# A tile's transpose turn in two halves, router turns of two tiles, and a new order at the end of a scan kernel

## The chip, the cores and the metric

The kernel runs on one core of one Trainium2 chip. The metric is the device time of one execution in microseconds (us). Before the change three timed runs gave 1213.72, 1214.86 and 1219.25 us, median 1214.86 us.

## The reference, cut to what matters

The input `x` is 2 sequences of 1024 tokens, 256 wide (2048 tokens). Two layers follow one another; each has a sequence part and a feed-forward part, both on a layer-normed input and with a residual:

```
# layer 0, attention part: a selective scan with state 64
xn    = norm(x) * norm_w + norm_b
proj  = xn @ x_proj_w.T                       # 128 + 64 + 64 columns
delta = softplus(proj[:, :128] @ dt_proj_w.T + dt_proj_b)
for each token:                               # per sequence
    h = exp(delta * A) * h + delta * B * xn   # h: 256 channels x 64 states
    y = sum over states of h * C
x = x + (y + x * D_param) @ out_proj_w.T
# layer 0, feed-forward part: mixture of experts
probs = softmax(norm(x) @ Wg)                 # 8 experts, the best 2 of each token
# place of a token in its expert = rank over all tokens; beyond CAP = 640 it is dropped
x = x + sum over 2 experts of gate * (relu(x_e @ w1[e]) @ w2[e])
# layer 1: linear attention with 16 heads, then a gated feed-forward part (silu)
```

A token's place in an expert depends on all tokens before it, so tokens are routed in order. The first expert can't start before every row that it takes has been written to its slot.

## The kernel before, in words

**Stages.** In the profiled execution the scan runs from about 32 to 626 us, the end of the scan stage with the last routing to about 658 us, the eight experts to about 960 us, and layer 1 to the end. The change is in the first two and in the loads of the first two experts.

**The scan stage.** The 2048 tokens are 32 chunks of 64 (`c`), and each chunk has 8 groups of 16 channels (`j`): 256 groups `gi = 8 c + j`. A tile is 128 tokens, two chunks. For each group TensorE makes the decay exponents (`decays`, L909, for group `gi + 2`) and the scan's inputs (L928); ScalarE takes the exponentials (L1089) and writes the carry of the chunk before into the inputs' first column (`hand_on`, L1097); GpSimd multiplies the carry (L1412 to L1421); VectorE runs one scan instruction of 1024 elements (L1266). TensorE's `stream(gi)` waits until the scan of group `gi - 2` is done, multiplies `unread[gi - 1]` products that nobody reads (`stay_awake`, L895), and then makes the inputs of `gi` and the decays of `gi + 2`.

**The order.** `scan_schedule()` (L619 to L733) writes one list of steps; each engine walks through this list and does its own part of every step, in order. Beside the groups there are: `y` (L944, the state times C, four steps per chunk, in groups 2, 3, 5 and 7), the finish of a tile (`TILE_END`, L566), the projections of later tokens (`unit_steps`, names that begin with `u_`) and the routing of finished tiles (`router_steps`, L576). `unread_after` (L736) counts the TensorE work of a group by `PE_WORK` and gives the group after it 3 unread products less that count, not below 0.

**The turns of bank z.** The eighth PSUM bank serves all side work in turns. A step of `Z_WRITE` opens it (TensorE writes) and its partner closes it (ScalarE or VectorE reads and counts up `z_free`). Router and unit turns open only in groups 4 and 6 of an even chunk and 1 and 3 of an odd one, and not between a tile's `yT` and its `resid`.

**A tile's finish.** `yT` turns the skipped input `xs` and the scan's output `y_sb` of both chunks (L979, L984) in one group, group 5 of an odd chunk; `yt` copies it (L1207, L1208), `proj` and `proj2` multiply by the output weights (L956), `resid` copies to `x1o` (L1215). `skip_in` makes `xs` on GpSimd.

**Routing.** Tiles go in blocks `ROUTED` of 4, 4, 4, 3 and 1 tiles. In a block each tile is transposed in one turn (`tr`, L1032, and `xt`, L1233) and multiplied by the router's weights in the next (`mm`, L1052), and ScalarE copies its logits away. Then come top 2 (`CHOOSE`), the gates (`WEIGH`), the ranks, the slots (`SETTLE`) and two indirect DMAs per tile from GpSimd (`scatter`, L1483). Block 2 (tiles 8 to 11) has its eight scatters from group 255 on. Blocks 3 (tiles 12 to 14) and 4 (tile 15) are routed after the last group in an order written out by hand (L707 to L733), in other banks.

**Behind the scan.** SP loads the weights of experts 0 and 1 (`load_experts`, 4 MB) behind the last group, waits for all scatters, and then loads the rows of expert 0 (L1673). TensorE runs `IDLE_ROUTED` = 14 unread products of 512 columns in the meantime (L553), so that the experts' first transposes (L1556) come next in its queue.

Of the kernel before, what the change touches and what calls it, by code (L numbers as in the profile page):

```python
# [7 lines left out]
P = 128  # L8
# [3 lines left out]
ALU = mybir.AluOpType  # L12
ACT = mybir.ActivationFunctionType
# [533 lines left out]
IDLE_ROUTED = 14  # L547
# [28 lines left out]
def router_steps(blk):  # L576
# [36 lines left out]
Z_WRITE = {"tr": "xt", "mm_last": "logit", "rank": "pick", "yT": "yt", "proj": "resid", "first": "first_out",  # L613
# [5 lines left out]
def scan_schedule():  # L619
# [7 lines left out]
    def stamp(name, *args):  # L627
# [8 lines left out]
        if name in ("mm", "proj2"):  # L636
            return (name, *args, z)
        return (name, *args)

    def advance(work, c=CHUNKS, j=4):  # L640
        if work:
# [3 lines left out]
            if steps[0] and steps[0][0][0] == "u_dt" and j > GROUPS - 3:  # L645
                return
# [19 lines left out]
    for gi in range(TOTAL + LAG):  # L666
# [8 lines left out]
        yield from advance(units, c, j)  # L675
        yield from advance(routing, c, j)
        if c >= CHUNKS - 4 and routing and not any(name in AT_PACE for name, *args in routing[0][1][0]):
            yield from advance(routing, c, j)
# [30 lines left out]
    yield ("skip_in", TILES - 1)  # L709
# [7 lines left out]
    yield stamp("yT", TILES - 1)  # L717
    yield stamp("yt", TILES - 1)
# [30 lines left out]
def selective_scan(k, a, s):  # L749
    pe, act, dve, pool, sp, sem = k.pe, k.act, k.dve, k.pool, k.sp, k.sem  # L750
    ident, eps, slots = s["ident"], s["eps"], s["slots"]
    with ExitStack() as ctx:
# [3 lines left out]
        logit_, top_, less_, prob_ = (sb("r_" + n, [P, NR, EXPERTS]) for n in ("logit", "top", "less", "prob"))  # L756
        hot_, own_ = sb("r_hot", [P, NR, 2, EXPERTS]), sb("r_own", [P, NR, 2, EXPERTS])
        xt = sb("r_xt", [P, 2, DH, P])
# [57 lines left out]
        xt_of = lambda blk, i: (last_xt[:, NR - 1 if blk == len(ROUTED) - 1 else i] if blk in ends else xt[:, i % 2])  # L816

        def on_sp():
# [8 lines left out]
            for kind, *x in schedule:  # L827
# [1485 lines left out]
```

## Time and profile before

| what | us |
|---|---|
| median of three timed runs | 1214.86 |
| profiled execution, device time | 1209.28 |
| its span, first to last instruction | 1207.7 |
| TensorE busy in the span | 1087.6 (90%) |
| VectorE busy | 761.2 (63%) |
| ScalarE busy | 519.3 (43%) |
| GpSimd busy | 323.7 (27%) |
| VectorE busy from 60 to 660 us | 561.02 of 600 |
| mean granted TensorE clock | 0.979 |

Busy time is the time in which an engine had an instruction under way. A mean over the span mixes stages: up to about 626 us VectorE is busy nearly all the time, behind 660 us TensorE is. Rows of the timeline give start, length, engine, line, operation and shape, and in square brackets how long the engine was idle before it and what ended that. Ends of matmuls are modelled.

### The profile page before, as it was taken

How to read it: one execution, taken by the hardware profiler on the slowest of the kernel's cores; microseconds unless marked ns; L12 is line 12 of the kernel's file. 1: busy time of each engine (PE TensorE's matmuls, PEld its weight loads, DVE VectorE, ACT ScalarE, POOL GpSimd, SP SyncE). 2: the span in 40 equal slices, each digit the busy share in tenths (PEclk: the TensorE clock that was granted, in tenths of full speed). 3: DMA queues.
4: the chain of work that ended last, by engine and by line, in shares of the span. 5: the costliest groups of instructions: out<-in, count | busy, mean ns of one | idle time of the engine just before them, and what ended most of it. 6: DMA issues, size and time to landing. Idle time of an engine off the chain costs nothing. (4 is left out here: it accounts for less than half of the span.)

```text
span 1207.7 us, 30229 instructions
## 1 busy us (share of the span) xinstructions
PE 1087.6 (90%) x12351; PEld 735.4 (61%) x12351; DVE 761.2 (63%) x874; ACT 519.3 (43%) x1344; POOL 323.7 (27%) x949
## 2 busy tenths in 40 slices
PE   3889888889888899888878999999999899999998
PEld 2655555556555565555544877788867666576465
DVE  5999999999999999999972112111111667242111
ACT  3777776776766767666541111111112212112110
POOL 5344444343345424443242110111111210000000
PEclk7899999999998999998998999999999999999999
DMA  6767747342353533523217622232110400000000
GB/s 159 165 161 175 176 107 197 64 109 74 77 123 86 119 66 70 126 62 71 37 56 273 258 107 102 74 110 109 56 47 20 140 1 1 1 18 9 9 18 18
DMA packets 183899, 110.11 MB, mean 91 GB/s; under 512 B 95517, under 2 KB 178336, under 8 KB 181408
## 3 DMA queue, kind: packets, MB, share of 16 engines
q1 hardware_dynamic: 178816, 98.65, 31.6%
q0 software_dynamic: 3456, 8.48, 2.0%
q8 instruction: 97, 1.59, 0.6%
q10 hardware_dynamic: 1488, 1.05, 0.4%
q14 instruction: 42, 0.34, 0.1%
HBM read 63.25 MB, written 43.90 MB: 89 GB/s over the span
## 5 line engine op out<-in xcount | busy, mean ns | idle before, releaser
L1266 DVE TENSOR_TENSOR_SCAN h<-decay,psum 128x1024 f32<-128x1024 f32 x256 | 564.8, 2266 | 18.1 <-ACT psum L1097 10.5
L1089 ACT ACTIVATE decay<-psum 128x512 f32<-128x512 f32 x512 | 278.6, 598 | 45.9 <-PE psum L909 43.0
L928 PEld LDWEIGHTS psum<-xdiag,bstat 128*128 128x128 bf16 x4096 | 148.4, 99 | 112.4 <-DVE h L1266 76.5
L928 PE MATMUL psum<-xdiag,bstat 128*128 128x64 bf16 x4096 | 166.5, 195 | 13.1 <-DVE h L1266 12.0
L1581 PE MATMUL psum<-shared,hid 128*128 128x256 f32 x640 | 139.7, 379 | 0.9 <-DVE hid L1660 0.9
L944 PE MATMUL psum<-h,cstat 128*32 128x512 f32 x1024 | 138.2, 614 | 2.3 <-DVE h L1266 1.7
L1569 PE MATMUL psum<-xdt,shared 128*128 128x320 f32 (+2 forms) x512 | 139.5, 433 | 0.8 <-ACT xdt L1632 0.8
L1581 PEld LDWEIGHTS psum<-shared,hid 128*128 128x128 f32 x640 | 120.9, 190 | 17.7 <-issue 1.7
L895 PE MATMUL psum<-shared 128*128 128x512 bf16 x262 | 74.3, 390 | 60.0 <-DVE h L1266 59.9
L1569 PEld LDWEIGHTS psum<-xdt,shared 128*128 128x128 f32 x512 | 92.3, 190 | 45.2 <-issue 15.3
L909 PE MATMUL psum<-rows,shared 32*128 32x64 bf16 x4096 | 106.0, 191 | 12.3 <-DMA rows<-parts_d 9.0
L1412 POOL TENSOR_TENSOR carry<-decay,h 128x16 f32<-128x16 f32 x240 | 58.1, 242 | 203.8 <-ACT decay L1089 201.6
L2190 PE MATMUL psum<-xt,wgu 128*128 128x512 f32 x256 | 110.6, 592 | 0.0
L1693 POOL DMA_INDIRECT picked_d<-eo,to x40 | 38.9, 972 | 255.2 <-ACT eo L1629 152.9
L1660 DVE TENSOR_SCALAR hid<-psum 128x320 f32<-128x320 f32 (+1 forms) x56 | 29.1, 520 | 103.9 <-PE psum L1569 103.9
L909 PEld LDWEIGHTS psum<-rows,shared 32*128 32x128 bf16 x4096 | 75.4, 94 | 27.1 <-issue 10.8
L1097 ACT COPY psum<-carry 128x16 f32<-128x16 f32 x240 | 43.4, 181 | 109.9 <-PE psum L928 90.6
L2190 PEld LDWEIGHTS psum<-xt,wgu 128*128 128x128 f32 x256 | 48.6, 190 | 59.7 <-issue 59.5
L1626 ACT ACTIVATE hid<-psum 128x320 f32<-128x320 f32 (+2 forms) x72 | 30.2, 419 | 117.7 <-PE psum L1569 117.7
L1663 DVE TENSOR_SCALAR eo<-psum,gate 128x256 f32<-128x256 f32 x19 | 9.2, 484 | 112.9 <-PE psum L1581 107.2
L1963 DVE TENSOR_TENSOR shared<-psum,sil 128x512 f32<-128x512 f32 x32 | 22.1, 690 | 86.0 <-PE psum L2190 86.0
L1418 POOL TENSOR_TENSOR carry<-carry,u 128x16 f32<-128x16 f32 x240 | 52.9, 220 | 84.2 <-ACT u L1126 67.7
(245 smaller groups left out, 1086.9 us busy)
## 6 DMA issues: line engine op xcount, KB each, us to landing
shared<-in_w SPq DMA_DIRECT2D x16, 1024.0 KB, 4.8
xdiag<-x_parts_d SPq DMA_DIRECT2D x124, 96.0 KB
rows<-parts_d SPq DMA_DIRECT2D x128, 48.0 KB
x_parts_d<-x_parts SPq DMA_DIRECT2D x14, 384.0 KB, 3.4
x_parts_d<-x_parts SPq DMA_DIRECT2D x21, 256.0 KB, 3.3
disp_d<-r_xl SPq DMA_DIRECT2D x4, 1305.0 KB, 8.5
xd<-disp_d SPq DMA_DIRECT2D x8, 652.5 KB, 6.1
picked_d<-r_xl SPq DMA_DIRECT2D x4, 1024.0 KB, 5.5
```

The costliest lines, as they stand in the source:

```text
L895: pe.q.matmul(bank, s["astat"][:, 0, :], s["astat"][:, 0:4, :].rearrange("p c m -> p (c m)"), start=True, stop=True)
L909: ins = pe.q.matmul(bank_a[half][:, i * T:(i + 1) * T], s["astat"][strip, RCH * g + q, :], rows[strip, c % 2, q, :], start=True, stop=True)
L928: ins = pe.q.matmul(to.rearrange("p d (s e) -> p s d e", e=2), bstat[:, c % 2, b, :], xdiag[:, c % 2, b, :, d, :], start=True, stop=True)
L944: ins = pe.q.matmul(bank_y[32 * q:32 * q + 32, :].rearrange("p (s d e) -> p s d e", s=2, e=4), s["cstat"][:, tok // 4, :], h[:, first:last ...
L1089: act.q.activation(decay[:, gi % NB, 8 * half:8 * half + 8, :], per_d(bank_a[half]), ACT.Exp).then_inc(sem("exp"), 1)
L1097: act.q.copy(per_d(bank_in[gi % 2])[:, :, 0], carry[:, gi % NB, :]).then_inc(sem("handed_on"), 1)
L1266: dve.q.tensor_tensor_scan(out=h[:, half_slot(c, half), ch:ch + G, :].rearrange("p d t -> p (d t)"), data0=decay[:, gi % NB, :, :].rearran ...
L1412: pool.q.tensor_tensor(whole, first, h[:, half_slot(c - 1, half), ch:ch + G, T - 1], ALU.mult).then_inc(sem("carry_made"), 1)
L1418: pool.q.tensor_tensor(whole.rearrange("p (h i) -> p h i", h=2), whole.rearrange("p (h i) -> p h i", h=2), own, ALU.add).then_inc(sem("car ...
L1569: ins = pe.q.matmul(table.bank(key)[:, 0:cols.stop - cols.start], w1[:, e % 2, dh, f * P:(f + 1) * P], xdt[:, e % 2, dh, cols], start=dh = ...
L1581: ins = pe.q.matmul(table.bank(key)[:, 0:D], hid[:, e % 2, f, st * P:(st + 1) * P], w2[:, e % 2, f, :], start=f == 0, stop=f == FT - 1)
L2190: ins = pe.q.matmul(table.bank(key)[:, :], wgu[:, j, dh, f * P:(f + 1) * P], xt[:, u, dh, :], start=dh == 0, stop=dh == 1)
```

## The change

It has five parts.

- `yT` does the first chunk of a tile in group 4 of the odd chunk, and a new step `yT2` the second in group 5. `PE_WORK` counts each as 2, so the unread products ahead of group 5 go from 3 to 1. A unit's `u_dt` no longer opens in group 3 of an odd chunk.
- Router turns take two tiles: `tr` makes four transposes and `xt` one copy of 512 columns; one `mm` step multiplies all tiles of the block (8 matmuls for 4 tiles), an empty step follows, and VectorE copies all logits at once. `PE_WORK` counts `tr` as 4; `mm` is not in it.
- Behind the last group: `skip_in` of tile 15 comes right after group 256's step instead of behind the eight scatters of block 2; blocks 3's `exp`, gates, slots and scatters come ahead of `resid` of tile 15 and of block 4.
- SP loads only `w1` of expert 0 behind the last group; the other three loads stand behind the experts' row loads.
- `IDLE_ROUTED` goes from 14 to 10. Some small tiles are shared (`r_less` with `r_prob`, `r_own` with `r_hot`), and `r_xt` has room for four tiles.

```diff
-IDLE_ROUTED = 14
+IDLE_ROUTED = 10
-PE_WORK = {"y": 4, "u_turn": 4, "u_proj": 6, "u_dt": 4, "u_tx": 4, "tr": 2, "yT": 4, "proj": 4}
+PE_WORK = {"y": 4, "u_turn": 4, "u_proj": 6, "u_dt": 4, "u_tx": 4, "tr": 4, "yT": 2, "yT2": 2, "proj": 4}
-TILE_END = ((4, 4, "yT"), (5, 5, "yt"), (8, 6, "proj"), (8, 6, "proj2"), (10, 8, "resid"))
+TILE_END = ((3, 3, "yT"), (4, 4, "yT2"), (5, 5, "yt"), (8, 6, "proj"), (8, 6, "proj2"), (10, 8, "resid"))
@@ router_steps
-    for i in range(n):
-        yield ([("mm", i - 1)] if i else []) + [("tr", i)]
+    for i in range(0, n, 2):
+        yield [("tr", i)]
         yield [("xt", i)]
-    yield [("mm_last", n - 1)]
+    yield [("mm",)]
+    yield []
@@ scan_schedule
-            if steps[0] and steps[0][0][0] == "u_dt" and j > GROUPS - 3:
+            if steps[0] and steps[0][0][0] == "u_dt" and (j > GROUPS - 3 or (c % CT and j == 3)):
...
+        if gi == TOTAL:
+            yield ("skip_in", TILES - 1)
...
-    yield from ((name, b3) for name in CHOOSE if name != "exp")
+    yield from ((name, b3) for name in CHOOSE)
     yield ("rank", b3)
+    yield from ((name, b3) for name in (*WEIGH, *SETTLE))
+    yield from (("scatter", b3, i, j) for i in range(ROUTED[b3][1]) for j in range(2))
     yield stamp("resid", TILES - 1)
     yield from ((name, b4) for name in NORM)
-    yield ("exp", b3)
+    yield ("count", b3)
     yield from (("turn", b4), ("turned", b4), ("score", b4, 0))
-    yield from ((name, b3) for name in (*WEIGH, *SETTLE, "count"))
-    yield from (("scatter", b3, i, j) for i in range(ROUTED[b3][1]) for j in range(2))
     yield from ((name, b4) for name in CHOOSE)
@@ on_sp, load_experts
-                    for e in range(2):
-                        for w, name in zip(expert_weights(s["shared"]), ("w1", "w2")):
-                            sp.q.dma_start(w[:, e], a[name][e]).then_inc(sem(f"w_expert{e}"), 16)
+                    w1, _ = expert_weights(s["shared"])
+                    sp.q.dma_start(w1[:, 0], a["w1"][0]).then_inc(sem("w1_ld0"), 16)
@@ on_pe: yT does th = 0, yT2 th = 1
-                    for th in range(CT):
-                        for dh in range(DH):
-                            pe.q.matmul(turned_in(th)[:, :, dh, :], xs[:, dh * P:(dh + 1) * P], ...
+                    for dh in range(DH):
+                        pe.q.matmul(turned_in(th)[:, :, dh, :], xs[:, dh * P:(dh + 1) * P], ...
@@ on_pe: tr
-                    for dh in range(DH):
-                        ins = pe.q.transpose(bank_z[:, dh * P:(dh + 1) * P], rows_of(blk)[:, i, dh * P:(dh + 1) * P], ident[:, :])
+                    for n in range(2 * DH):
+                        j, dh = divmod(n, DH)
+                        ins = pe.q.transpose(bank_z[:, n * P:(n + 1) * P], rows_of(blk)[:, i + j, dh * P:(dh + 1) * P], ident[:, :])
@@ on_act: xt
-                    if i:
-                        act.q.copy(logit_[:, ROUTED[blk][0] % NR + i - 1, :], logits_at(blk)[:, EXPERTS * (i - 1):EXPERTS * i])
-                    act.q.copy(xt_of(*x[0:2]).rearrange("p h t -> p (h t)"), bank_z[:, 0:2 * P]).then_inc(sem("z_free"), 1)
+                    i = x[1]
+                    act.q.copy(xt[:, i:i + 2].rearrange("p i h t -> p (i h t)"), bank_z).then_inc(sem("z_free"), 1)
@@ experts, on_sp
         load(0)
+        sp.q.dma_start(w2[:, 0], a["w2"][0]).then_inc(sem("w2_ld0"), 16)
         load(1)
+        sp.q.dma_start(w1[:, 1], a["w1"][1]).then_inc(sem("w1_ld1"), 16)
+        sp.q.dma_start(w2[:, 1], a["w2"][1]).then_inc(sem("w2_ld1"), 16)
         later()
```

## Rows read from the trace of the kernel before

**Rows 1.** Groups by line: busy us, mean ns; idle us before them, by releaser.

```profile
L1266 DVE TENSOR_TENSOR_SCAN h<-decay,psum 128x1024 f32<-128x1024 f32 x256 | 564.8, 2266 | 18.1 <-ACT psum L1097 10.5 <-PE psum L928 7.0
```

**Rows 2.** Timeline of VectorE, scan stage: start us, us; in brackets idle before.

```profile
135.43 34.95 DVE L1266 TENSOR_TENSOR_SCAN h<-decay,psum 128x1024 f32<-128x1024 f32 x16 [0.67 <-ACT psum L1097]
...
355.33 18.45 DVE L1266 TENSOR_TENSOR_SCAN h<-decay,psum 128x1024 f32<-128x1024 f32 x8 [0.45 <-ACT psum L1097]
...
552.93 1.38 DVE L1314 TENSOR_SCALAR r_xl<-x1o,r_mom,r_rstd 128x256 f32<-128x256 f32 x4 [0.91 <-DMA disp_d<-r_xl,slots]
...
563.99 17.53 DVE L1266 TENSOR_TENSOR_SCAN h<-decay,psum 128x1024 f32<-128x1024 f32 x8 [0.88 <-ACT psum L1097]
...
582.19 13.18 DVE L1266 TENSOR_TENSOR_SCAN h<-decay,psum 128x1024 f32<-128x1024 f32 x6 [0.67 <-ACT psum L1097]
...
623.64 2.29 DVE L1266 TENSOR_TENSOR_SCAN h<-decay,psum 128x1024 f32<-128x1024 f32 x1 [0.56 <-PE psum L928]
```

**Rows 3.** Timeline of TensorE, groups 5 and 6 of chunk 21.

```profile
391.93 0.82 PE L895 MATMUL psum<-shared 128*128 128x512 bf16 x3 [1.20 <-DVE h L1266]
392.59 0.63 PE L928 MATMUL psum<-xdiag,bstat 128*128 128x64 bf16 x16
...
393.49 1.06 PE L944 MATMUL psum<-h,cstat 128*32 128x512 f32 x8
394.48 0.66 PE L979 MATMUL psum<-ident,xs 128*128 128x64 f32 x4
...
395.92 0.63 PE L928 MATMUL psum<-xdiag,bstat 128*128 128x64 bf16 x16
```

**Rows 4.** Timeline of TensorE: one tile's router product.

```profile
262.99 0.61 PE L1052 MATMUL psum<-r_wg,r_xt 128*128 128x8 f32 x4
```

**Rows 5.** One stretch: busy us by engine, granted clock, DMA share, GB/s.

```profile
556.84:560.26 3.42, 3.29 (x54) 2.35 (x51) 3.42 (x2) 1.53 (x4) 0.59 (x3) 0.50 0.08 24
```

**Rows 6.** Timeline of TensorE around the last scan.

```profile
621.62 0.63 PE L928 MATMUL psum<-xdiag,bstat 128*128 128x64 bf16 x16
622.17 1.06 PE L944 MATMUL psum<-h,cstat 128*32 128x512 f32 x8
...
626.41 3.64 PE L944 MATMUL psum<-h,cstat 128*32 128x512 f32 x32 [1.68 <-DVE h L1266]
...
632.13 0.84 PE L1042 MATMUL psum<-ident,decay 128*128 128x128 f32 x6 [2.07 <-DVE decay L1314]
```

**Rows 7.** Timeline of ScalarE around the last scan.

```profile
623.33 0.18 ACT L1097 COPY psum<-carry 128x16 f32<-128x16 f32 x1 [2.78 <-PE psum L928]
...
628.33 0.37 ACT L1215 COPY x1o<-psum 128x256 f32<-128x256 f32 x1 [2.06 <-remote]
...
631.63 0.77 ACT L1140 COPY y_raw<-psum 128x128 f32<-128x128 f32 x4 [0.90 <-remote]
```

**Rows 8.** Timeline of VectorE, routing of tiles 12 to 15.

```profile
637.81 0.18 DVE L1352 TENSOR_TENSOR r_ind<-r_hot 128x24 bf16<-128x24 f32 x1
638.06 0.43 DVE L1297 BATCH_NORM_STATS2 r_stats<-x1o 128x6 f32<-128x256 f32 x1
...
639.69 0.17 DVE L1355 TENSOR_REDUCE r_total<-r_prob 128x3 f32<-128x24 f32 x1
...
641.09 0.16 DVE L1385 TENSOR_TENSOR slots<-r_at,r_over 128x6 uint32<-128x6 f32 x1
```

**Rows 9.** Timeline of GpSimd, the last scatters.

```profile
642.03 1.06 POOL L1483 DMA_INDIRECT disp_d<-decay,slots  x1 [10.84 <-DVE slots L1385]
...
651.03 0.97 POOL L1483 DMA_INDIRECT disp_d<-decay,slots  x1 [0.30 <-issue]
...
653.53 0.11 POOL L1698 MEMSET xl<- 128x8 f32 x1 [1.53 <-DMA disp_d<-decay,slots]
```

**Rows 10.** Timeline of TensorE: unread products, then the experts' first transposes.

```profile
642.83 15.33 PE L553 MATMUL psum<-ident 128*128 128x512 f32 x28
...
658.24 1.31 PE L1556 MATMUL psum<-ident,xd 128*128 128x128 f32 x10
```

More of the change, by code:

```diff
@@ L610, in unit_steps @@
     yield [("u_store_x", 2)]
-Z_WRITE = {"tr": "xt", "mm_last": "logit", "rank": "pick", "yT": "yt", "proj": "resid", "first": "first_out",
+Z_WRITE = {"tr": "xt", "mm": "logit", "rank": "pick", "yT": "yt", "proj": "resid", "first": "first_out",
            "u_turn": "u_xn", "u_proj": "u_take", "u_dt": "u_relu", "u_tx": "u_xhi"}
@@ L675, in scan_schedule @@
         yield from advance(units, c, j)
+        if gi == TOTAL:
+            yield ("skip_in", TILES - 1)
         yield from advance(routing, c, j)
-        if c >= CHUNKS - 4 and routing and not any(name in AT_PACE for name, *args in routing[0][1][0]):
+        if c >= CHUNKS - 4 and routing and routing[0][1][0] and not any(name in AT_PACE for name, *args in routing[0][1][0]):
             yield from advance(routing, c, j)
@@ L755, in selective_scan @@
         x1o, xl = sb("x1o", [P, NR, D]), s["xl"]
-        logit_, top_, less_, prob_ = (sb("r_" + n, [P, NR, EXPERTS]) for n in ("logit", "top", "less", "prob"))
-        hot_, own_ = sb("r_hot", [P, NR, 2, EXPERTS]), sb("r_own", [P, NR, 2, EXPERTS])
-        xt = sb("r_xt", [P, 2, DH, P])
+        logit_, top_, prob_ = (sb("r_" + n, [P, NR, EXPERTS]) for n in ("logit", "top", "prob"))
+        hot_ = sb("r_hot", [P, NR, 2, EXPERTS])
+        xt = sb("r_xt", [P, NR, DH, P])
         tri_f, tri = xl[:, 0, 0:2 * P].rearrange("p (a b) -> p a b", b=P), sb("r_tri", [P, 2, P], BF16)
@@ L1044, in on_pe @@
                     ins.then_inc(sem("r_turn"), 1)
-                elif kind in ("mm", "mm_last", "score"):
-                    blk, i = x[0:2]
+                elif kind in ("mm", "score"):
+                    blk = x[0]
                     if kind == "score":
                         pe.wait_ge(sem("r_turned"), blk - len(ROUTED) + 3)
+                        done = x[1:2]
                     else:
-                        pe.wait_ge(sem("z_free"), x[2])
-                    for dh in range(DH):
-                        ins = pe.q.matmul(logits_at(blk)[:, EXPERTS * i:EXPERTS * (i + 1)], xt_of(blk, i)[:, dh, :],
-                                          wg[:, dh, :], start=dh == 0, stop=dh == 1)
+                        pe.wait_ge(sem("z_free"), x[1])
+                        done = range(ROUTED[blk][1])
+                    for i in done:
+                        for dh in range(DH):
+                            ins = pe.q.matmul(logits_at(blk)[:, EXPERTS * i:EXPERTS * (i + 1)], xt_of(blk, i)[:, dh, :],
+                                              wg[:, dh, :], start=dh == 0, stop=dh == 1)
                     if i == ROUTED[blk][1] - 1:
@@ L1281, in on_dve @@
                     continue
-                if kind.startswith("u_") or kind in ("resid", "skip_in", "y", "y_out", "y_sel", "yT", "yt", "proj", "load_parts", "load_epilogue", "load_experts",
+                if kind.startswith("u_") or kind in ("resid", "skip_in", "y", "y_out", "y_sel", "yT", "yT2", "yt", "proj", "load_parts", "load_epilogue", "load_experts",
                             "load_weights", "zero_slots", "proj2", "first",
@@ L1288, in on_dve @@
                 at, n3, tiles = first % NR, n * EXPERTS, slice(first, first + n)
-                logit, less, prob, top, hot, own_place, ind = (
-                    v[:, at:at + n] for v in (logit_, less_, prob_, top_, hot_, own_, ind_))
+                logit, prob, top, hot, ind = (v[:, at:at + n] for v in (logit_, prob_, top_, hot_, ind_))
                 share, where, kept, over, slot_at = (v[:, at:at + n, :] for v in (share_, where_, kept_, over_, at_))
@@ L1375, in on_dve @@
                         dve.wait_ge(sem("z_free"), z_pick)
[L1376 removed]
+                    done(dve.q.tensor_reduce(where, hot, AX.X, ALU.add))
                 elif kind == "kept":
```

53 lines of the change are left out of this document (25 added, 28 removed).

## The prediction

> **What bounds the kernel now.** I read the page's busy times first, then the groups by line, then VectorE's timeline of the scan stage and, at each gap in it, TensorE's; last the timelines of all engines around the last scan. The scan line shows 256 scans of VectorE with 18.1 us idle before them, of which 10.5 us end with ScalarE's carry copy L1097 [rows 1]. The timeline shows sixteen scans in 34.95 us without a gap, 2.18 us each, and then a gap of 0.67 us [rows 2]. So VectorE bounds the scan stage, and once per tile something makes it wait. There are 18 such gaps. Thirteen stand before the scan that follows a tile's `yT`: 0.46, nine times 0.67, 1.03, 0.45 and 0.36, together 8.3 us; the other five, 2.2 us, are 0.18, 0.26, 0.54, 0.88 and 0.35. TensorE at such a place [rows 3]: unread products from 391.93, inputs from 392.59, decays, `y` from 393.49, `yT` from 394.48 to 395.92, and only then the next group's inputs. It was idle 1.20 us before this group, and late at its end. Behind the last scan the bound is a chain over all engines (state product, normalisation, router, slots, scatters, the load of expert 0), and from 658 us TensorE.
>
> **The gap as a sum.** In rows 3 the unread products take 0.66, `y` and `yT` 0.99 + 1.44 = 2.43 us; with no unread ones before the next group that is 3.09 us beside the fixed work, and the gap was 0.67. So a group may hold 3.09 - 0.67 = 2.42 us of such work, with the unread products of the next group counted in, before VectorE waits.
>
> **The two halves.** Group 5 now holds one unread product (0.22), `y` (0.99) and half of `yT` (0.72): 1.93, under 2.42. Group 4 was empty and gets 0.72 plus the 0.22 after it. Both fit, the thirteen gaps go: -8.3 us. ScalarE's `yt` stays in group 6 and no longer finds its input late. What would be late next is `y_sel` of the odd chunk; its copy is issued two groups earlier, and `yT` never waited for it. Bounds: 0 if the second half still ends late, -8.3.
>
> **Router turns.** Two tiles take four transposes in one turn and one wider copy on ScalarE, in groups that hold at most a `y` step beside them; hidden. The product is not: one tile's took 0.47 us (0.61 with its tail [rows 4]), four take 1.88 us in one step. In blocks 0 and 1 it falls in group 1 of an odd chunk, behind three unread products, and as `mm` is not in `PE_WORK` three more follow: 0.66 + 1.88 + 0.66 = 3.20, which is 0.78 over 2.42. In block 2 it falls in group 4 of chunk 28 behind a `y`: 1.88 + 0.66 = 2.54, 0.12 over. Together +1.7 us. Bounds: 0 and +2.5. VectorE's logit copy is two groups behind the product because of the empty step, so it does not wait. The routing ends earlier: block 1's last scatter goes from group 225 to 200, and block 2's normalisation to group 216. Its wait of 0.91 us for the scatters [rows 2] goes: -0.9 (0 if ScalarE's `rstd` is late in its place).
>
> **Block 2's scatters** move from groups 255 and later into groups 248 to 255, one per group. Block 0's scatters already run so, and eight scans there took 18.45 us where eight others took 17.53 [rows 2]: +0.9; I take +0.8, between that and block 1's, where I saw none. Bounds 0 and +2.
>
> **The clock.** After VectorE's pauses for a block's statistics and normalisation TensorE has little to do and the granted clock falls to 0.50 [rows 5], that is 1.2 of 2.4 GHz; the gap of 0.88 us at 563.99 [rows 2] lies in such a stretch. After the change two-tile turns and halves of `yT` come right behind block 2's normalisation, so a stretch at the low level holds more work. I take +1.0; bounds -0.9 (no such stretch) and +3.4.
>
> **The last scan.** The gap of 0.56 us before it [rows 2] I count as gone, -0.6: it is the late end of TensorE's inputs, whose records end at 622.25 while the carry copy that waits for them starts at 623.33 [rows 6, 7]. Scan stage: -8.3 + 1.7 - 0.9 + 0.8 + 1.0 - 0.6 = -6.3 us.
>
> **Behind the last scan.** The last scan ends at 625.93 [rows 2]; the transposes of tiles 12 to 14 start at 632.13 [rows 6], 6.2 us later. They wait for a normalisation that starts from `x1o` of tile 14, copied at 628.33 [rows 7] though its product's records end near 624.7. The same lateness shows at L1140: 631.63, where the 32 state products end at 630.05 by their records [rows 6, 7]. TensorE was some 2 to 3.6 us behind its records while GpSimd issued block 2's eight scatters back to back until 629.8. With those in the loop, the state products start about 0.5 us behind the last scan and take 3.5 (3.64 by rows 6), and the transposes start at +4.0 instead of +6.2: -2.2 us. `x1o` is copied at about the last scan's end, and its normalisation then takes the 3.3 us it took, so it is ready before. Bounds 0 and -2.2. `skip_in` of tile 15, 1.4 us of GpSimd, was not waited for and is not now.
>
> **Block 3 ahead of block 4.** Block 3's slots come at 641.25 because VectorE first does tile 15's statistics and normalisation: 638.06 to 639.69 [rows 8]. In the new order its sums start behind `r_ind` at 637.99 and take the 1.56 us that they took (639.69 to 641.25): 639.55, -1.7 us. ScalarE's `exp` is now ahead of `resid`, and ready. GpSimd's eight scatters take 642.03 to 652.0 [rows 9] back to back; the six of block 3 fill 7.65 us, and tile 15's slots, some 6 us behind, arrive in time. So the end of all scatters moves by the whole 1.7. Bounds -1.0 and -1.75.
>
> **Free edits.** Loading `w1` of expert 0 alone leaves 3 MB for behind the rows; `w2` of expert 0 is needed 20 us after the rows and the next expert's weights 36 us after. If a load were late, TensorE would stand still by that much; experts start on the rows alone, as before. Sharing small tiles adds no wait. Unit 2's deferral by some groups has more than one chunk of slack before its first load.
>
> **Fewer unread products.** 28 records of 14 products end at 658.17, and the transposes start at 658.24 [rows 10]. The rows' load follows the scatters (653.53 [rows 9]) by 4.6 us and now ends 1.7 us earlier relative to that chain. Ten products take at least 4 x 0.85 = 3.4 us less, but start some 1.4 us later in the chain, so they end up to 2 us before the rows land. No gain by itself; 0, bound +3.4 if the clock falls there.
>
> Here the Trainium skill speaks against my reading. "SBUF — State Buffer", section "SBUF: two separate sides", says that a DMA and a compute operation can't slow each other and that TensorE's own port never waits for anyone. By that rule scatters can't be what makes TensorE late, the 2.2 us behind the last scan would stay, as would the 0.6, and the 0.8 in the loop would not appear. The trace does not agree so far: the late ends of rows 6 and 7 lie under back-to-back scatters.
>
> **Sum.** -6.3 - 2.2 - 1.7 = -10.2 us on the profiled execution's 1209.28 (span 1207.7): 1199.1. The median of the timed runs stands 5.6 us above that execution; I keep this distance: 1214.86 - 10.2 = 1204.7 us.
>
> **Rivals.**
> A. TensorE's lateness has another cause than scatters and stays. -8.3 + 1.7 - 0.9 + 1.0 - 1.7 = -8.2, 1206.7 us. For: the gap before the last scan is put down to TensorE alone, and eight scans beside block 1's scatters lost nothing. Against: away from scatters ScalarE's copies start within 0.1 us of the records' ends.
> B. The experts start at the low clock, since TensorE is idle between its ten products and the rows. The 14 products took 15.33 us [rows 10], 3.4 more than 14 of 0.85, since the clock was at 0.50 from 642.2 to 649.0; such a stretch among the experts costs as much: 1208.1 us. For: fewer products. Against: the idle time is short.
> C. The low clock and the four-tile product eat the scan's gain: +3.4 instead of +1.0, +2.5 instead of +1.7, and TensorE's lateness stays: -10.2 + 2.4 + 0.8 + 2.2 = -4.8, 1210.1 us.
> D. The halves don't do what they say: the second waits for `y_sel` or `xs`, the gaps stay: -1.9, 1213 us. Against: neither wait shows before.
> E. Slower: with 2 unread products less per tile the clock falls once per tile. At the price of the one stretch seen, 0.88 us, fifteen cost 13.2: 1217.9 us. It decides from 12 such stretches on. For: the low stretches come where TensorE has pauses. Against: `yT` in group 4 is work in a group that had none.
>
> **Chances.** Forecast 0.45, A 0.18, B 0.12, C 0.13, D 0.06, E 0.06. 0.5% is 6.1 us, about what a measurement of this kernel tells from no change: below 1208.8 it is faster. Forecast and A are faster nearly always, B mostly, C seldom: 0.77; within 0.5% 0.17; slower 0.06. The range from 1200 to 1211 takes in the forecast with its bounds, A, B and C, and leaves out D and E and a gain of over 15 us.
>
> **What would show it.** VectorE's timeline: gaps of 0.67 us once per 16 scans gone, two new ones of about 0.8 us behind `mm` steps. The last scan's end near 619.6. L1042 about 4 us behind it; slots of block 3 some 7.4 us behind L1042's start, last scatter's end near 641.8, the experts' first transposes near 648, and unchanged spans from there. The prediction is wrong if the gaps stay, if the granted clock falls in more stretches of the scan than the four it has between 40 and 626 us, or if the experts' stage is longer.

## The result, and the profile after

| | before | after |
|---|---|---|
| median of six timed runs each, same chip | 1213.76 us | 1205.07 us |
| lowest and highest | 1207.76 to 1219.25 | 1197.76 to 1209.11 |
| ratio | | 0.9938, 95% interval 0.9914 to 0.9962 |
| a second series (25 and 8 runs) | 1212.08 us | 1202.78 us |
| ratio | | 0.9927, interval 0.9900 to 0.9953 |

The change makes the kernel 0.6 to 0.7% faster, 7.5 to 8.8 us by the two ratios. The forecast was 10.2 us less and 1204.7 us. The ratios here and below are those on record with each series and not the quotients of the medians shown, from which they differ by up to 0.2%; gains in us are worked out from the ratios.

The two profiled executions do not show that gain: the span of before is 1207.7 us, that of after 1207.8. Each is one draw. The profiled execution of after took 1209.11 us and is the slowest of its six; the second profile of after, taken later, is the slowest of its eight (1207.59 us). That of before took 1209.28 us, 2.8 to 4.5 us under the medians of before in these two series. So the stages have to be compared one by one. The line of the scan in the groups of after, which answers to [rows 1]:

```profile
span 1207.8 us, 30068 instructions
L1271 DVE TENSOR_TENSOR_SCAN h<-decay,psum 128x1024 f32<-128x1024 f32 x256 | 565.9, 2267 | 22.1 <-ACT psum L1104 13.9
```

VectorE waits 22.1 us ahead of its scans, where [rows 1] had 18.1: there is more idle time although the gaps once per tile are gone. TensorE's timeline shows for tile 8 that they are. It answers to [rows 3]: both are groups 4 and 5 of chunk 19, counted from the scans ([rows 3] says chunk 21, which is a slip). The first half of `yT` stands behind group 4's inputs, the second behind group 5's `y`:

```profile
391.59 0.66 PE L981 MATMUL psum<-ident,xs 128*128 128x64 f32 x4 [0.29 <-ACT r_xt L1238]
392.08 0.44 PE L986 MATMUL psum<-ident,y_sb 128*128 128x128 f32 x2
392.57 0.63 PE L930 MATMUL psum<-xdiag,bstat 128*128 128x64 bf16 x16
...
393.47 1.07 PE L946 MATMUL psum<-h,cstat 128*32 128x512 f32 x8
394.47 0.66 PE L981 MATMUL psum<-ident,xs 128*128 128x64 f32 x4
394.96 0.44 PE L986 MATMUL psum<-ident,y_sb 128*128 128x128 f32 x2
395.24 0.63 PE L930 MATMUL psum<-xdiag,bstat 128*128 128x64 bf16 x16
```

VectorE's timeline over the same tile, and over the product that follows it, shows both sides: fourteen scans without a gap, and then the four-tile product. (The 0.64 us ahead of the fourteen follow a stretch at the low clock that ends at 386.7 us and a turn of four transposes. This scan, 156, is 0.25 to 0.79 us late in the four profiles that have both, on time in those that have one of the two or neither.)

```profile
391.74 30.71 DVE L1271 TENSOR_TENSOR_SCAN h<-decay,psum 128x1024 f32<-128x1024 f32 x14 [0.64 <-ACT psum L1104]
422.37 0.17 DVE L1328 COPY r_logit<-psum 128x32 f32<-128x32 f32 x1
424.80 2.29 DVE L1271 TENSOR_TENSOR_SCAN h<-decay,psum 128x1024 f32<-128x1024 f32 x1 [2.26 <-ACT psum L1104]
427.00 0.35 DVE L1337 MAX8 r_top<-r_logit 128x8 f32<-128x8 f32 x4
428.15 2.29 DVE L1271 TENSOR_TENSOR_SCAN h<-decay,psum 128x1024 f32<-128x1024 f32 x1 [0.80 <-ACT psum L1104]
```

TensorE there, and the window of that stretch (busy us of each engine, the granted clock, the share of DMA):

```profile
419.71 2.60 PE L1059 MATMUL psum<-r_wg,r_xt 128*128 128x8 f32 x16
422.55 1.06 PE L897 MATMUL psum<-shared 128*128 128x512 bf16 x2 [0.23 <-DVE h L1271]
423.40 1.06 PE L930 MATMUL psum<-xdiag,bstat 128*128 128x64 bf16 x16
```

```profile
420.80:427.60 6.80, 6.57 (x66) 4.13 (x66) 4.29 (x7) 1.37 (x4) 2.73 (x9) 0.50 0.59 180
```

The product has 16 records of 8 columns. It took 2.60 us where the same product at full clock took 1.95 (`after_again` below): the clock fell to 0.50 in it, and for 6.8 us a group's inputs took 1.01 to 1.06 us instead of 0.63. The VectorE gaps are 2.26 and 0.80 us.

Behind the last scan, which ends at 630.38, the rows of after that answer to [rows 6, 8 and 9] are these. First TensorE, then VectorE, then GpSimd:

```profile
630.43 3.64 PE L946 MATMUL psum<-h,cstat 128*32 128x512 f32 x32 [1.01 <-DVE h L1271]
634.01 0.88 PE L1046 MATMUL psum<-ident,decay 128*128 128x128 f32 x6
...
646.66 10.24 PE L553 MATMUL psum<-ident 128*128 128x512 f32 x20
658.25 1.31 PE L1557 MATMUL psum<-ident,xd 128*128 128x128 f32 x10 [1.36 <-DMA xd<-disp_d]
```

```profile
641.27 0.16 DVE L1389 TENSOR_TENSOR slots<-r_at,r_over 128x6 uint32<-128x6 f32 x1
641.35 0.42 DVE L1301 BATCH_NORM_STATS2 r_stats<-x1o 128x6 f32<-128x256 f32 x1
```

```profile
642.21 1.05 POOL L1487 DMA_INDIRECT disp_d<-decay,slots  x1 [11.29 <-DVE slots L1389]
...
651.22 0.97 POOL L1487 DMA_INDIRECT disp_d<-decay,slots  x1 [0.30 <-issue]
653.78 0.11 POOL L1702 MEMSET xl<- 128x8 f32 x1 [1.59 <-DMA disp_d<-decay,slots]
```

The slots of block 3 are ready 7.4 us behind the start of the transposes, and tile 15's statistics now come after them.

**Where the time is, kernel by kernel.** The table takes every kernel's profile apart in the same way. Two scans in a row start 2.178 us apart where nothing is in the way, and 2.20 us at some places. The table takes 2.191 for all, in each kernel alike, so the columns can be compared but "rest" is up to 3 us too small in every row. What each start is later than 2.191 is its excess. The excess is put down to the scan behind a tile's `yT` ("tile"), to a scan that meets a stretch at the granted clock 0.50 ("low clock"), to the groups with scatters where VectorE has no routing work of its own ("scatters"), and to all else ("rest", most of it VectorE's own routing work; the gap behind the product is in it). The clock comes first where several hold, so "low clock" also holds work of VectorE, a product or a scatter that would have cost something at full clock too. 255 times 2.191 and the last scan's 2.29 make 561.0 us; with the sum of the row that is the scan stage.

| kernel | scan stage | tile | low clock | scatters | rest | last scan to L1042 | last scan to the experts |
|---|---|---|---|---|---|---|---|
| before | 593.7 | 9.4 | 5.4 | 1.2 | 16.7 | 6.2 | 32.3 |
| before, again | 592.6 | 8.7 | 6.2 | 0.4 | 16.3 | 3.6 | 33.2 |
| after | 597.8 | 2.2 | 14.2 | 3.8 | 16.6 | 3.6 | 27.9 |
| after, again | 596.6 | 2.2 | 13.4 | 2.7 | 17.3 | 3.6 | 28.0 |
| halves | 582.8 | 0.8 | 4.0 | 0.6 | 16.4 | 3.6 | 31.3 |
| router | 599.8 | 8.6 | 10.1 | 3.2 | 16.9 | 3.6 | 30.3 |
| tail | 593.2 | 9.7 | 5.8 | 0.4 | 16.4 | 3.6 | 28.1 |
| halves_tail | 585.3 | 1.0 | 7.7 | 0.6 | 15.0 | 3.6 | 29.2 |
| halves_tail14 | 583.7 | 1.4 | 4.0 | 0.6 | 16.7 | 3.6 | 30.6 |
| after_held | 588.9 | 1.7 | 10.6 | 0.1 | 15.5 | 3.6 | 27.8 |
| after_counted | 586.6 | 2.3 | 3.1 | 3.5 | 16.7 | 3.6 | 27.8 |
| best | 588.4 | 2.1 | 11.9 | 0.1 | 13.3 | 3.6 | 28.0 |

From the experts' first transposes to the end all take 549.0 to 549.9 us, but for `tail` with 550.7.

### The profile page after: what moved, and what is told of

The parts are those of the page before. It is cut to its first block and busy times, and to the rows that moved or that the text cites. A ratio compares the mean times of both kernels' runs of the same rounds, so it can differ in the third digit from the quotient of the medians.

```text
span 1207.8 us, 30068 instructions
## 1 busy us (share of the span) xinstructions
PE 1073.0 (89%) x12238; PEld 738.3 (61%) x12318; DVE 761.8 (63%) x874; ACT 518.2 (43%) x1329; POOL 325.1 (27%) x949
## 5 line engine op out<-in xcount | busy, mean ns | idle before, releaser
L1271 DVE TENSOR_TENSOR_SCAN h<-decay,psum 128x1024 f32<-128x1024 f32 x256 | 565.9, 2267 | 22.1 <-ACT psum L1104 13.9
L930 PE MATMUL psum<-xdiag,bstat 128*128 128x64 bf16 x4096 | 168.9, 196 | 16.7 <-DVE h L1271 14.6
L897 PE MATMUL psum<-shared 128*128 128x512 bf16 x157 | 49.5, 404 | 68.2 <-DVE h L1271 66.9
L911 PEld LDWEIGHTS psum<-rows,shared 32*128 32x128 bf16 x4096 | 76.1, 95 | 27.9 <-issue 9.7
L1967 DVE TENSOR_TENSOR shared<-psum,sil 128x512 f32<-128x512 f32 x32 | 22.1, 689 | 86.0 <-PE psum L2194 86.0
```

The costliest lines, as they stand in the source:

```text
L897: pe.q.matmul(bank, s["astat"][:, 0, :], s["astat"][:, 0:4, :].rearrange("p c m -> p (c m)"), start=True, stop=True)
L911: ins = pe.q.matmul(bank_a[half][:, i * T:(i + 1) * T], s["astat"][strip, RCH * g + q, :], rows[strip, c % 2, q, :], start=True, stop=True)
L930: ins = pe.q.matmul(to.rearrange("p d (s e) -> p s d e", e=2), bstat[:, c % 2, b, :], xdiag[:, c % 2, b, :, d, :], start=True, stop=True)
L1271: dve.q.tensor_tensor_scan(out=h[:, half_slot(c, half), ch:ch + G, :].rearrange("p d t -> p (d t)"), data0=decay[:, gi % NB, :, :].rearran ...
```

## The experiments

"Before" in each comparison is the kernel before on the same chip: 1212.08 us for the first four, 1210.07 for the next four, 1212.43 for the last two.

**after_again: the changed kernel a second time.** No edit.

> The changed kernel itself, to see how much of its profile is its own and how much the execution's. In the first profile the scan ended 4.5 us later than before (630.4 against 625.9 us) and the stage behind it was 4.4 us shorter, so the span was the same, while the medians differ by 8.7. Theory 1 (the scan stage's length hangs on how many stretches at the low clock an execution happens to have; 44 us of them in that profile, 20 before): this profile has fewer and the scan ends by 626 or earlier; time 0.990 to 0.996 of before. Theory 2 (the scan stage is longer by the change itself, through GpSimd's queue and the four-tile product): the scan ends near 630 again, and the gain is the 4.4 us behind it, ratio 0.9965.

Measured 1202.78 us, ratio 0.9927 (0.9900 to 0.9953). Its profile agrees with the first in each place: tile gaps 2.2, low clock 13.4, scatters 2.7, 28.0 us from the last scan to the experts. The scan ends at 628.9 us, near what Theory 2 said; the ratio is that of Theory 1. So neither holds whole. At 268.81 it has the product at full clock, 1.95 us long, and VectorE's gap behind it:

```profile
268.81 1.95 PE L1059 MATMUL psum<-r_wg,r_xt 128*128 128x8 f32 x16
270.61 0.81 PE L897 MATMUL psum<-shared 128*128 128x512 bf16 x3
```

```profile
272.23 2.29 DVE L1271 TENSOR_TENSOR_SCAN h<-decay,psum 128x1024 f32<-128x1024 f32 x1 [0.60 <-ACT psum L1104]
```

**halves: only `yT` in two halves**, on the kernel before.

```
-PE_WORK = {..., "tr": 2, "yT": 4, "proj": 4}
+PE_WORK = {..., "tr": 2, "yT": 2, "yT2": 2, "proj": 4}
-TILE_END = ((4, 4, "yT"), (5, 5, "yt"), ...
+TILE_END = ((3, 3, "yT"), (4, 4, "yT2"), (5, 5, "yt"), ...
...
```

The delay of a unit's `u_dt` belongs to it.

> The kernel before with the tile's turn in two halves alone (router, tail and loads as before). Theory 1 (forecast): the gaps of 0.67 us once per tile go, 8.3 us less stretches at the low clock: -5 to -8 us. Rival (two unread products less per tile let the clock fall once per tile, each about 0.9 us): no gain or a loss; the profile would show ten or more low stretches in the scan.

Measured 1198.53 us, ratio 0.9908 (0.9884 to 0.9932), 11 us less. That is beyond the 5 to 8 of Theory 1, and more than the whole change by its middle value; the intervals overlap. Its profile has three stretches at the low clock between 40 us and the last scan, 17.1 us, where the rival wanted ten or more: the rival does not hold. The scan line's idle time falls to 10.9 us, and most of it now ends with TensorE's inputs, no longer with ScalarE's carry copy:

```profile
L1268 DVE TENSOR_TENSOR_SCAN h<-decay,psum 128x1024 f32<-128x1024 f32 x256 | 563.5, 2262 | 10.9 <-PE psum L929 6.5
```

**router: only the router turns of two tiles**, on the kernel before.

```
-    for i in range(n):
-        yield ([("mm", i - 1)] if i else []) + [("tr", i)]
+    for i in range(0, n, 2):
+        yield [("tr", i)]
         yield [("xt", i)]
-    yield [("mm_last", n - 1)]
+    yield [("mm",)]
+    yield []
```

> The kernel before with the two-tile router turns alone. Theory 1: the four-tile product costs two gaps of 0.8 us, block 1's scatters fall on unit 7's work on GpSimd and cost 2 us more, scatters in the last groups cost 0.2 us each by GpSimd's own time (2.39 us per group against 2.19), and TensorE's lateness behind the last scan goes (-2.2): together +1 to +4 us. Rival (fewer turns relieve TensorE and ScalarE): -2 us or better, without new gaps.

Measured 1211.83 us, ratio 1.0007 (0.9988 to 1.0025): no difference, just under the 1 to 4 us more of Theory 1; the rival's 2 us less lie outside the interval. The profile shows what it buys and what it pays. Against the two profiles of before the scatters' column has 3.2 instead of 0.8, the low clock 10.1 instead of 5.8, and the stretch behind the last scan is 2 to 3 us shorter. Block 2's scatters are no longer there, and TensorE no longer waits for `xs`, as it does for 1.57 us in `before_again` (below).

**tail: only the new end.** Block 3 to its scatters ahead of tile 15, `skip_in` of tile 15 right behind the last group, 10 unread products, only `w1` of expert 0 ahead of the rows. The main lines:

```
+        if gi == TOTAL:
+            yield ("skip_in", TILES - 1)
+    yield from ((name, b3) for name in (*WEIGH, *SETTLE))
+    yield from (("scatter", b3, i, j) for i in range(ROUTED[b3][1]) for j in range(2))
     yield stamp("resid", TILES - 1)
```

> The kernel before with the tail alone: block 3 ahead of block 4, skip_in of tile 15 earlier, only w1 of expert 0 loaded behind the last group, 10 unread products. Theory 1: slots of block 3 come 1.7 us earlier behind the transposes and all else follows; block 2's scatters stay back to back behind the last group, so TensorE stays late there (transposes 6.2 us behind the last scan): -1.7 us. Rival (the 4 MB of weight loads, not the scatters, made the chain late): transposes come at 4.0 us and the time is -3.5 to -4 us.

Measured 1205.86 us, ratio 0.9951 (0.9935 to 0.9968), 5.9 us less. From the last scan to the experts it takes 28.1 us instead of 32.3 and 33.2. That is more than either theory. The transposes stand at +3.6 us, as the rival said, but its cause is not shown by that: `before_again` has the 4 MB of loads and +3.6 us as well. In this execution rival B came: TensorE was idle 1.46 us before the experts' first transposes, and the next stretch ran at the low clock (550.7 us to the end against 549.4):

```profile
653.58 1.31 PE L1553 MATMUL psum<-ident,xd 128*128 128x128 f32 x10 [1.46 <-DMA xd<-disp_d]
```

```profile
655.50:658.90 3.40, 3.24 (x6) 2.19 (x7) 0.48 (x5) 0.44 (x1) 0.00 (x0) 0.50 1.09 404
```

**halves_tail: the halves and the new end, router turns as before.** The two edits above together.

> The kernel before with the halves of yT and the new tail, and the router turns left at one tile each. Theory 1 (the two-tile router turns are what the whole change pays for in the scan): the scan stage is that of the halves alone, about 583 us, the stretch from the last scan to the experts that of the tail alone, about 28 us, and the rest as before: 13.5 + 4.0 = 17.5 us less than the profile of before, or about 1195 us as a median, some 8 us under the whole change. Theory 2 (the parts hinder one another whatever the router does, by SP's loads or by the clock): no more than the whole change gives, about 1203 us.

Measured 1197.99 us, ratio 0.9889 (0.9867 to 0.9911), 13.4 us less. That is Theory 1 but for 3 us by the median and 4 by the ratio: the profile has 585.3 and 29.2 us for the two stretches, where 583 and 28 were expected, with 7.7 us at the low clock instead of the 4.0 of `halves`. Its median ratio lies 0.4 to 0.5% under those of the whole change; the interval ends below the one of the first series and overlaps that of the second by 0.1%. So the router turns of two tiles, which gained nothing alone, are not needed for the gain.

**halves_tail14: the same with 14 unread products.** `IDLE_ROUTED = 14` instead of 10.

> The same with 14 unread products of 512 columns ahead of the experts instead of 10, which fill TensorE until the rows of expert 0 land. If the experts pay for a stretch at the low clock behind ten products (rival B of the prediction), this is 1 to 1.5 us faster than the version with ten. If the low clock there is chance, the two are equal. If the fourteen end behind the rows, it is slower by what they stand over, up to 2 us.

Measured 1199.41 us, ratio 0.9908 (0.9887 to 0.9930): not told apart from the version with ten. Its end takes 30.6 us instead of 29.2 and its experts 549.0 instead of 549.5. The fourteen products stand over: GpSimd's `xl` (L1700), which follows the scatters, is at 639.82, and the experts start 6.8 us behind it, where the version with ten needs 4.4 (642.24 to 646.63) and waits for the rows. TensorE of the version with fourteen:

```profile
632.42 14.35 PE L553 MATMUL psum<-ident 128*128 128x512 f32 x28
646.61 1.25 PE L1555 MATMUL psum<-ident,xd 128*128 128x128 f32 x10
```

The price of B, 1.3 us seen once in `tail`, is not worth four products.

**after_held: the whole change, with scatters kept out of groups in which GpSimd has other work.**

```
+GP_STEPS = ("u_norm", "u_sum", "u_dtx", "u_dtrest", "u_dtlo", "u_xrest", "u_xlo")
-        yield from advance(units, c, j)
+        own = list(advance(units, c, j))
+        yield from own
+        hold = routing and routing[0][1][0] and routing[0][1][0][0][0] == "scatter" and gi < TOTAL and (
+            any(name in GP_STEPS for name, *_ in own) or (c % CT and j == 1))
...
-        yield from advance(routing, c, j)
+        if not hold:
+            yield from advance(routing, c, j)
```

> The whole change, but no scatter is issued in a group in which GpSimd has work of a unit or skip_in; the scatters of blocks 0 and 1 spread over a few more groups (blocks 1: 193 to 205), block 2's go to groups 248 and 250 to 256. Theory 1 (GpSimd is where scatters cost the scan): the gaps of 0.95, 0.90 and 0.21 us at scans 200 to 202 and of 1.0 us at scan 250 go, and 0.2 us remains per group with a scatter: 3 us less than the whole change. Theory 2 (the router turns cost by the clock and by the four-tile product alone): no difference beyond 1 us.

Measured 1198.52 us, ratio 0.9892 (0.9872 to 0.9912), 13.1 us less than before and so some 5 less than the whole change by the ratios (2.6 by the quotients of the medians; the interval overlaps that of the second series). The profiles give some 3 us: the scatters' column goes from 3.8 and 2.7 to 0.1. GpSimd at block 1's scatters in after, where groups hold a scatter and a unit's operation as well:

```profile
490.34 0.25 POOL L1416 TENSOR_TENSOR carry<-decay,h 128x16 f32<-128x16 f32 x1
490.67 0.22 POOL L1422 TENSOR_TENSOR carry<-carry,u 128x16 f32<-128x16 f32 x1
490.95 0.13 POOL L1425 MEMSET decay<- 128x16 f32 x1
491.07 1.16 POOL L1471 TENSOR_TENSOR dt_lo<-uxn,dt_low 128x512 bf16<-128x512 f32 x1
492.38 1.02 POOL L1487 DMA_INDIRECT disp_d<-r_xl,slots  x1 [0.15 <-issue]
493.42 0.26 POOL L1416 TENSOR_TENSOR carry<-decay,h 128x16 f32<-128x16 f32 x1
```

From one carry to the next 3.08 us go by, and a scan has 2.18. VectorE waits 0.88 and 0.80 us there:

```profile
494.50 2.29 DVE L1271 TENSOR_TENSOR_SCAN h<-decay,psum 128x1024 f32<-128x1024 f32 x1 [0.88 <-ACT psum L1104]
497.59 4.69 DVE L1271 TENSOR_TENSOR_SCAN h<-decay,psum 128x1024 f32<-128x1024 f32 x2 [0.80 <-ACT psum L1104]
```

VectorE at the same place of `after_held`:

```profile
477.07 24.08 DVE L1276 TENSOR_TENSOR_SCAN h<-decay,psum 128x1024 f32<-128x1024 f32 x11
```

Theory 1 holds in the profile, and more came than it said: block 2's 0.2 us per group went as well. The rows of GpSimd there show why:

```profile
612.09 1.02 POOL L1492 DMA_INDIRECT disp_d<-r_xl,slots  x1 [0.60 <-DVE h L1276]
613.15 0.25 POOL L1421 TENSOR_TENSOR carry<-decay,h 128x16 f32<-128x16 f32 x1
...
614.48 1.02 POOL L1492 DMA_INDIRECT disp_d<-r_xl,slots  x1 [0.60 <-DVE h L1276]
615.54 0.25 POOL L1421 TENSOR_TENSOR carry<-decay,h 128x16 f32<-128x16 f32 x1
```

A group with a scatter takes GpSimd 2.39 us (613.15 to 615.54), 0.2 more than a scan. GpSimd runs ahead of the need, so the first such groups are free: in `after_held` only scans 254 and 255 are late, by 0.20 us each (254 stands behind a `yT` and so in the column "tile"). In after, `skip_in`'s 1.3 us behind the second scatter eats that lead at once, and each scatter behind it costs 0.2. VectorE of after, the gap before scan 250:

```profile
616.09 14.29 DVE L1271 TENSOR_TENSOR_SCAN h<-decay,psum 128x1024 f32<-128x1024 f32 x6 [0.95 <-ACT psum L1104]
```

**after_counted: the whole change, with the product counted.** `PE_WORK` gets `"mm": 8`, so that no unread product stands behind it.

> The whole change, but the four-tile product counts as 8 in PE_WORK, so that no unread product stands behind it in the next group. At full clock each of the three products then leaves TensorE 0.66 us earlier: the gaps of 0.75 us behind those of blocks 0 and 1 shrink to about 0.1, 1.3 us less in all. If the product costs mainly because it falls in a stretch at the low clock (2.4 and 0.9 us at scans 170 and 171), then either such stretches come as before and the gain is up to 3 us there, or the missing unread products bring the clock down more often and nothing is gained.

Measured 1199.70 us, ratio 0.9910 (0.9877 to 0.9944); the interval is too wide to tell it from the whole change. The profile shows what it does: the excess of scans 106 and 170, behind the products of blocks 0 and 1, is 0.10 and 0.10 us; in `after_again` it was 0.75 at full clock and 2.29 at the low one. The two 0.65 us are the 1.3 that were expected. The low clock took 3.1 us in this execution.

**best: both repairs.**

> The whole change with both repairs: the four-tile product counts as 8 in PE_WORK, and no scatter is issued in a group in which GpSimd has work of a unit or skip_in. Theory (the products' 0.65 us each and GpSimd's 5 us are separate gaps of the scan, and neither brings the other): the scan stage is about 5 us shorter than with the product counted alone (586.6 us), so about 582 us, the experts start 27.8 us behind the last scan as in the whole change, and the median is about 1195 us, a ratio of 0.987. Rival: with more groups short of work for TensorE the clock falls more often and eats it; then the low-clock time in the scan is over 30 us and the median is that of the two repairs alone, 1199 us.

Measured 1197.30 us, ratio 0.9881 (0.9844 to 0.9917). The median is between theory and rival. The scatters' column stays at 0.1, so the repairs do not disturb one another. But the low clock is back at 11.9 us, with 34.1 us of stretches between 40 us and the last scan, and in one of them lies the product of block 0 (scan 106, excess 1.73), with no unread products behind it. So counting the product does not always keep the clock up; one profile each way does not say whether it helps, and the 3.1 us of `after_counted` may be chance. `best`, `halves_tail` and `after_held` are equal within their intervals. All three beat before, and their ratios are 0.4 to 0.5% under the mean of the whole change's two, with intervals that overlap at the edges.

**before_again: the kernel before, profiled a second time.**

> The kernel before, unchanged, for a second profile of it. If TensorE's lateness behind the last scan (transposes of tiles 12 to 14 at +6.2 us) belongs to this kernel, because its eight scatters are issued back to back there (the prediction's reading), it comes again at +6 us. If it was peculiar to the one execution that was profiled, the transposes stand at +3.6 us as in all other kernels profiled here, two of which (the halves alone, the tail alone) issue the same eight scatters there; then 2.6 us of the forecast gain were never to be had, and the profile of before sat that much above what it was read for. The time is that of before, a ratio of 1 within 0.3%.

Measured 1211.43 us, ratio 1.0002 (0.9976 to 1.0028). TensorE and GpSimd behind its last scan, which ends at 624.58 (they answer to [rows 6 and 7]):

```profile
624.63 3.64 PE L944 MATMUL psum<-h,cstat 128*32 128x512 f32 x32 [0.58 <-DVE h L1266]
628.21 0.88 PE L1042 MATMUL psum<-ident,decay 128*128 128x128 f32 x6
630.65 0.63 PE L979 MATMUL psum<-ident,xs 128*128 128x64 f32 x4 [1.57 <-POOL xs L1430]
```

```profile
628.14 0.97 POOL L1483 DMA_INDIRECT disp_d<-r_xl,slots  x1 [0.30 <-issue]
629.14 0.56 POOL L1427 TENSOR_SCALAR xs<-xres,mean_neg,rstd 128x256 f32<-128x256 f32 x1
629.79 0.72 POOL L1430 TENSOR_TENSOR xs<-xs,drow 128x256 f32<-128x256 f32 x1
```

The transposes stand at +3.6 us with the same eight scatters back to back. `x1o` is copied at 624.09, before the last scan's end, and not 2.4 us behind it as in [rows 7]. The other ten profiles all have +3.6 us, and four of them (`halves`, `tail` and the two of `halves_tail`) issue scatters back to back there too. The lateness was seen in the first profile alone. What this kernel does wait for there, and the first profile hid, is `skip_in` behind the scatters: 1.57 us (1.20 in `halves`). The kernels with `skip_in` ahead of the scatters, or with the scatters in the loop, have no such wait.

## Why the prediction was right, and where it was not

The median came within 0.4 us of the forecast, and the gain was 7.5 to 8.8 us where it said 10.2. That closeness is in good part luck. The forecast had the scan stage 6.3 us shorter, with its end near 619.6 us and the experts' first transposes near 648. Both profiles of after have the scan stage 3 to 5 us longer than those of before, its end at 630.4 and 628.9, and the transposes at 658.3 and 657.0. One of the prediction's own signs of being wrong came true in them: seven and six stretches at the low clock between 40 us and the last scan, where before has four in either profile. That the medians still gain what they do says that these two executions were worse than the usual one of after, and both are the slowest of their series. Some steps were right in cause and size; others were wrong in cause or size, and their errors went against each other.

**The gaps once per tile, -8.3: right.** In `halves` the column "tile" goes from 9.4 and 8.7 to 0.8 us, which is most of the 11 us that this kernel wins. In after it goes to 2.2, so 6.9 us are gained. The budget of 2.42 us per group held. One gap stays: tile 3's, 0.8 to 1.7 us in all kernels with halves. In after the second half waits there 1.51 us for `y_sb`, which is rival D in one tile of sixteen:

```profile
204.33 0.49 PE L986 MATMUL psum<-ident,y_sb 128*128 128x128 f32 x2 [1.51 <-DMA y_sb<-y_raw]
```

**The four-tile product, +1.7: right at full clock.** It was forecast at 0.78 in blocks 0 and 1, and the scan behind it is 0.75 late; block 2's costs nothing, where 0.12 was said. The sum didn't price that the product itself may lie at the low clock. There 0.75 became 2.3 to 2.4 in the two profiles of after (3.1 in `after_held`), and the next scan had 1.2 instead of 0.3.

**Block 2's wait for the scatters, -0.9: right.** It is 0.91 and 0.85 us in before and gone in all six profiles with the new router turns. (In the three with halves and without those turns it is 0.1 to 0.2 us.)

**Scatters in the loop, +0.8 for block 2 and nothing for block 1: too small.** In after the scans 200 to 202 (block 1) lose 0.95, 0.90 and 0.21, and the scans 250 to 255 (block 2) 1.02 and five times 0.20 to 0.24: 4.1 us together, of which 0.2 stand in the column "tile". The step named the queue that the scatters are moved into, but not what stands in it at that time: unit 7's operations of 1.1 to 1.3 us, and `skip_in`. GpSimd, at 27% busy over the span, is full in these groups. `after_held` shows it.

**The low clock, +1.0 with a bound of +3.4: too small in the profiles, open in the medians.** Both profiles of after have 13 to 14 us in that column against 5 to 6 in before, 8 us more. About 4 us of the one and 2 of the other are excess that the same scans have at full clock in other profiles. By this estimate the clock itself costs some 10 us in after and 4 in before: 6 us more, still outside the bound. This is the mechanism of rival C.

The usual execution can't have all of it. Without the column, the differences from the mean of before's two profiles are -6.9 (tile), +2.5 (scatters), +0.5 (rest) and -4.8 (behind the last scan), together -8.7 us, and the medians give -7.5 and -8.8. With the share put back that is not the clock's, the sum is some -6.7. The table sets the same sum, without the column, beside the measured difference (ratio less one, times the median of before).

| kernel | sum of the profile's columns | measured |
|---|---|---|
| halves | -10.0 | -11.2 |
| router | -0.1 | +0.8 |
| tail | -4.5 | -5.9 |
| halves_tail | -13.3 | -13.4 |
| halves_tail14 | -9.8 | -11.1 |
| after_held | -14.0 | -13.1 |
| after_counted | -8.8 | -10.9 |
| best | -15.6 | -14.4 |

They agree within about 2 us, and the intervals are at least as wide.

The mean granted clock of the timed runs does not settle it: 0.975 and 0.977 in the two series of after, 0.979, 0.977 and 0.976 in three series of before. In the profiles this mean depends as much on a stretch before 40 us, which is 20 to 24 us long or missing altogether: before has 0.979 with 20.5 us of stretches in the scan and 20.5 before 40 us, `tail` 0.987 with 20.5 and none, after 0.977 with 44.4 and none. The six profiles without router turns of two tiles have 4.0 to 7.7 us in the column, the six with them 10.1 to 14.2, except `after_counted` with 3.1. In five of those six a stretch lies at a four-tile product or within 3 us of it (266 to 276 us, or 419 to 428), and in one of the other six at that place. That speaks for the wider turns drawing such stretches, but it is not shown, and what they cost in the usual execution stays open.

**The 0.6 before the last scan and the 2.2 behind it: the cause was wrong.** The step read a late TensorE beside back-to-back scatters and made the one the cause of the other. (By its own rows the lateness was 3.6 us at `x1o` and 1.6 at L1140, not 2 to 3.6.) `before_again`, `halves`, `tail` and the two of `halves_tail` have the scatters and +3.6 us; it was rival A, and in the form that the lateness belonged to one execution only. What made it late there is not known. The sum of this part came out nearly right because the change takes away another wait that the first profile did not show: the wait for `skip_in`, 1.57 us. The prediction had said of it that it was not waited for. From the last scan to the experts the forecast was -3.9; measured are -4.4 against the first profile of before and -5.2 against the second.

The Trainium skill's rule from the prediction ("SBUF — State Buffer", section "SBUF: two separate sides": a transfer can't slow TensorE's own port) agrees with these runs: same scatters, +3.6 us. The prediction took from the rule too that the scatters' 0.8 us in the loop would not appear. That did not follow: they appeared, 4.1 us, and not through TensorE. Its page "DMA: Bandwidth & Descriptors", section "SWDGE vs HWDGE vs iDMA", says that a DMA issued from GpSimd has its descriptors computed by a program on GpSimd; the trace fits that, with 1.02 us of GpSimd busy for each scatter. What the scan paid for is this time in GpSimd's queue.

**Block 3 ahead of block 4, -1.7: right.** The slots come 7.4 us behind L1042's start, as forecast, and the scatters fill the same 10 us. **Free edits and fewer products: right**, the experts' stage is unchanged (549.4 and 549.6), and the ten products end 1.4 us before the rows land, where up to 2 was said; rival B showed once, in `tail`, for 1.3 us instead of 3.4. Rival E, which wanted 12 stretches or more, came in no profile: the most is seven.

## What to carry to other kernels

A long step of TensorE's queue may be cut in two wherever the group next to it has room; the room can be read from one gap as work minus gap. When small steps are moved in time, lay them against the timeline of the queue that they go into, group by group: an engine at 27% on the page can be full in the one group that matters, and a rule of a few lines that keeps them off such groups was worth some 3 us here by the profiles and 3 to 5 by the medians. Try the parts of a change alone: here two of them did all the work. And profile the kernel before twice before a wait seen once becomes a term of a sum.

## What the runs showed of the hardware

An indirect DMA of GpSimd keeps it busy for 1.02 to 1.06 us and mostly stands 0.60 us behind the operation before it in the scan loop (`after`, `after_held`); when eight follow one another it is 0.97 us busy with 0.30 us between (`before_again`).

The granted clock's stretches at 0.50 differ between executions of one kernel. Between 40 us and the last scan the two profiles of before have four each, 20.5 and 17.1 us in all: at 222.3, 379.4, 556.8 and 601.2 in one, at 234.6, 381.4, 528.2 and 558.9 in the other. Two of the four overlap, the others lie elsewhere. The two profiles of after have 44.4 and 37.5 us.
